# Eight-wide attentions of a twelve-layer decoder: half of the first pair's keys and queries laid by DMA instead of by products, and the rows rearranged for it

## What is computed

```python
q = (queries @ Wq + bq).reshape(b, s, 16, 8)
k = (context @ Wk + bk).reshape(b, p, 16, 8)
v = (context @ Wv + bv).reshape(b, p, 16, 8)
scores = einsum('bqhd,bkhd->bhqk', q, k) / sqrt(8)     # + mask in L0_attn and L1_xattn
out = einsum('bhqk,bkhd->bqhd', softmax(scores), v).reshape(b, s, 128) @ Wo + bo
```

## Time and profile before

| | |
|---|---|
| median of 3 runs | 1826.79 us (1822.91 to 1831.64) |
| the profiled execution, its own time | 1836.73 us |
| its span | 1834.7 us |
| busy PE / DVE / ACT / POOL | 76% / 67% / 50% / 18% of the span |
| granted TensorE clock, mean | 0.878 |

### The profile page before, as it was taken

How to read it: one execution, slowest core, us unless ns; L and a number is a source line. 1 busy time by engine, 2 the same in 40 slices (tenths; PEclk the granted TensorE clock), 3 DMA queues, 4 the chain that set the end, 5 groups by cost and what they waited for, 6 DMA issues and landing times. The chain is left out here.

```text
span 1834.7 us, 31839 instructions
## 1 busy us (share of the span) xinstructions
PE 1388.5 (76%) x10614; PEld 859.6 (47%) x10630; DVE 1235.9 (67%) x4823; ACT 920.4 (50%) x2002; POOL 337.9 (18%) x360
## 2 busy tenths in 40 slices
PE   5897978872874768895455799999983995777874
PEld 2454434441763543442234456666653883443442
DVE  7888368865336768887666677677764224657887
ACT  4654357641322336655622577777751442136666
POOL 3320022112524124400021000000002333303100
PEclk9999999985996879997567799999995997679997
DMA  3230014211561012310010000000003672003300
GB/s 126 55 53 2 0 22 54 36 35 48 164 125 40 12 52 49 51 25 20 1 59 1 12 7 7 12 7 7 1 2 110 186 203 59 23 18 49 55 4 24
DMA packets 59362, 83.42 MB, mean 45 GB/s; under 512 B 8065, under 2 KB 46209, under 8 KB 58689
## 3 DMA queue, kind: packets, MB, share of 16 engines
q1 hardware_dynamic: 54208, 71.15, 15.7%
q0 software_dynamic: 4992, 10.23, 3.0%
HBM read 51.18 MB, written 9.18 MB: 33 GB/s over the span
## 5 line engine op out<-in xcount | busy, mean ns | idle before, releaser
L873 ACT ACTIVATE L_xattn_probs<-ps 128x1024 f32<-128x1024 f32 x192 | 196.5, 1024 | 73.7 <-PE ps L1066 68.9
L714 DVE TENSOR_REDUCE maxs<-ps 128x4 f32<-128x1024 f32 x128 | 156.5, 1222 | 29.7 <-PE ps L1042 29.6
L3467 ACT ACTIVATE wide_pr<-wide_sc,wide_nm 128x256 f32<-128x256 f32 x256 | 127.0, 497 | 13.3 <-DVE wide_nm L3395 12.7
L1543 POOL DMA_INDIRECT moe_xs<-normed,moe_table x92 | 87.1, 947 | 156.7 <-PE ps L1573 73.9
L1042 PE MATMUL ps<-keys,L_xattn_qs 64*128 64x256 bf16 x768 | 75.3, 274 | 53.5 <-DVE maxs L714 33.3
L1082 PE MATMUL ps<-L_xattn_probs,values 128*32 128x256 f32 x1536 | 102.8, 385 | 0.0
L708 DVE CUSTOM_DVE_ANT_0 L_xattn_masked_scores<-ps,L_xattn_maskQ 128x256 bf16<-128x256 f32 x256 | 93.1, 420 | 14.1 <-PE ps L1042 14.1
L3390 DVE COPY wide_prT<-ps 128x512 f32<-128x512 f32 x64 | 44.3, 692 | 84.5 <-PE ps L3508 84.4
L3365 DVE CUSTOM_DVE_ANT_0 wide_sc<-ps,wide_mask 128x256 f32<-128x256 f32 x256 | 93.2, 419 | 3.3 <-PE ps L3493 2.2
L1972 DVE SCALAR_TENSOR_TENSOR moe_z_sb<-ps,moe_wt,moe_a_sb 128x256 f32<-128x256 f32 x46 | 22.3, 484 | 93.4 <-ACT moe_a_sb L2003 78.5
L708 DVE CUSTOM_DVE_ANT_0 L_attn_masked_scores<-ps,L_attn_maskQ 128x128 bf16<-128x128 f32 (+1 forms) x256 | 76.0, 353 | 7.6 <-PE ps L1042 7.2
(11 more groups left out here) (625 smaller groups left out, 3604.9 us busy)
## 6 DMA issues: line engine op xcount, KB each, us to landing
moe_wt<-in_packed_experts SPq DMA_DIRECT2D x23, 707.0 KB
moe_wt<-in_packed_experts SPq DMA_DIRECT2D x23, 384.0 KB
keys<-L_xattn_k_parts SPq DMA_DIRECT2D x108, 64.0 KB
L_xattn_qs<-L_xattn_q_parts SPq DMA_DIRECT2D x108, 64.0 KB
expert_out<-moe_y SPq DMA_DIRECT2D x46, 128.0 KB
weights<-in_packed_L_xattn SPq DMA_DIRECT2D x2, 1316.0 KB, 7.2
keys<-L_attn_k_parts SPq DMA_DIRECT2D x36, 64.0 KB
L_attn_qs<-L_attn_q_parts SPq DMA_DIRECT2D x36, 64.0 KB
```

What stands on the lines that cost most here:

```text
L714: v.tensor_reduce(nm, ps[:, BANK_M:BANK_M + 2, :].rearrange("p j (t n) -> p j t n", t=2), AX.X, ALU.max, negate=True).then_inc(S("m_used"), 1)
L873: a.activation(probs[:, s % RING, :, :, :].rearrange("p j t n -> p j (t n)"), ps[:, BANK_P:BANK_P + 2, :], ACT.Exp, scale=HD ** -0.5)\
L1543: g.indirect_dma_start(self.xs[:, j % BUFS, h * P:(h + 1) * P], None, C.normed, bass.IndirectOffsetOnAxis(self.table[:, n:n + 1], 0))\
L3467: ins = a.activation(pr[:, s % 3, j, qt, :], sc[:, s % 2, j, qt, :], ACT.Exp, bias=nm[:, s % 2, n:n + 1], accum_out=sums[:, s % 2, n:n + 1])
```

## The change

For pair 0, only groups 0 to 3 are placed by products (`PLACED` = 4); groups 4 to 7 of keys and queries are laid by transfers, `lay_keys(sp, 0)` and `lay_queries(sp, 0)`, 12 DMAs each. So that the rows of groups 4 to 7 are contiguous in a part, the column order becomes (head of the group, half of the groups, element, group in its half). A transfer can now cover only 32 contiguous rows for 4 groups; pairs 1 to 3 need both halves, so their layings are 24 DMAs of 32 KB each instead of 12 of 64 KB. Slots 4 to 7 wait for `k_laid` and `q_laid` of 192, and slot 16 m for 192 + 384 m. DVE's copies of keys 4 to 7 and ACT's of queries 4 to 7 go. The spare rows of pair 0's groups 4 to 7 are cleared by two more DMAs in each attention, and set once by two more memsets; the selection matrices are made by 12 copies of half the size instead of 6 on each of DVE and ACT.

```diff
+    PLACED = GP // 2
-    KEY_BANKS = (BANK_P, BANK_P + 1, BANK_T, BANK_V, BANK_P, BANK_P + 1, BANK_P, BANK_P + 1)
-    KEYS_AT = (-2, -2, -1, -1)
+    KEY_BANKS = (BANK_P, BANK_P + 1, BANK_T, BANK_V)
@@ parts_free
-                eng.wait_ge(S(("queries_placed", "keys_placed")[n]), GP)
-            elif m > 2:
-                eng.wait_ge(S(("q_laid", "k_laid")[n]), 192 * (m - 2))
+                eng.wait_ge(S(("queries_placed", "keys_placed")[n]), PLACED)
+            if m >= 2:
+                eng.wait_ge(S(("q_laid", "k_laid")[n]), laid(m - 2))
@@
+        def unplaced(m):
+
+            return range(2) if m else (1,)
+
+        def laid(m):
+
+            return 192 + 384 * m
@@ lay_keys (lay_queries likewise)
-                    eng.dma_start(kk[r0:r0 + HD, m % 2, :, :], parts(m, 1, part)[half[j]]).then_inc(S("k_laid"), 16)
+                    for h in unplaced(m):
+                        rows = slice(64 * j + 32 * h, 64 * j + 32 * h + 32)
+                        eng.dma_start(kk[r0:r0 + HD, m % 2, PLACED * h:PLACED * (h + 1), :], parts(m, 1, part)[rows])\
+                           .then_inc(S("k_laid"), 16)
@@ lay_queries
-            if m == 1:
-                eng.wait_ge(S("rows_cleared"), 32)
+            if m < 2:
+                eng.wait_ge(S("rows_cleared"), 64)
@@ SP queue
                 for m in range(PAIRS):
-                    if m:
-                        lay_keys(sp, m)
+                    lay_keys(sp, m)
                     if boundary is not None:
                         turn_masks(sp, m)
-                    if m:
-                        lay_queries(sp, m)
+                    lay_queries(sp, m)
@@ DVE: copy_key and its two calls are removed
@@ ACT
-                for gp in range(GP // 2):
+                for gp in range(PLACED):
...
-                    if 0 <= s - QUERIES_AT - 1 < GP:
+                    if 0 <= s - QUERIES_AT - 1 < PLACED:
@@ PE, max_scores
                     if s < GP:
-                        pe.wait_ge(S("q_ready"), gp + 1)
+                        query_copied(pe, gp)
                         key_copied(pe, gp)
...
-                            pe.wait_ge(S("k_laid"), 192 * m)
-                            pe.wait_ge(S("q_laid"), 192 * m)
+                            pe.wait_ge(S("k_laid"), laid(m))
+                            pe.wait_ge(S("q_laid"), laid(m))
@@ PE, places
-                    if 0 <= s - QUERIES_AT < GP:
+                    if 0 <= s - QUERIES_AT < PLACED:
                         place_query(s - QUERIES_AT)
-                    for n, t in enumerate(KEYS_AT):
-                        if s == t:
-                            place_key(GP // 2 + n)
@@ decoder
+                L(g.memset(C.keys[96:128, 0, HEADS // 4:, :], 1.0))
...
+                L.tick(v.memset(C.keys[32:64, 0, HEADS // 4:, :], 1.0))
...
-                for slot in range(len(K_PARTS)):
-                    dst, one = lay_rows(1, slot)
+                for slot, h in product(range(len(K_PARTS)), range(2)):
+                    dst, one = lay_rows(1, slot, h)
                     L.tick(v.tensor_copy(dst, one))
@@ by_rows
-    return np.ascontiguousarray(wt.reshape(wt.shape[0], HEADS // 2, 2, HD).transpose(0, 2, 3, 1)).reshape(wt.shape)
+    return np.ascontiguousarray(wt.reshape(wt.shape[0], 2, HEADS // 4, 2, HD).transpose(0, 3, 1, 4, 2)).reshape(wt.shape)
```

More of the change, by code:

```diff
@@ L8 @@
 import itertools
+from itertools import product
 from contextlib import ExitStack, contextmanager
@@ L432, in parts_free, with query_copied @@
             if m == 2:
-                eng.wait_ge(S(("queries_placed", "keys_placed")[n]), GP)
-            elif m > 2:
-                eng.wait_ge(S(("q_laid", "k_laid")[n]), 192 * (m - 2))
+                eng.wait_ge(S(("queries_placed", "keys_placed")[n]), PLACED)
+            if m >= 2:
+                eng.wait_ge(S(("q_laid", "k_laid")[n]), laid(m - 2))
         def key_copied(eng, gp):
-            eng.wait_ge(S("later_keys" if gp >= GP // 2 else "early_keys"), gp % (GP // 2) + 1)
+            if gp < PLACED:
+                eng.wait_ge(S("early_keys"), gp + 1)
+            else:
+                eng.wait_ge(S("k_laid"), laid(0))
+        def query_copied(eng, gp):
+            if gp < PLACED:
+                eng.wait_ge(S("q_ready"), gp + 1)
+            else:
+                eng.wait_ge(S("q_laid"), laid(0))
+        def unplaced(m):
+            return range(2) if m else (1,)
+        def laid(m):
+            return 192 + 384 * m
         places = [Place(tau, WINDOW, PAIRS) for tau in range(-WINDOW, SLOTS + 13)]
@@ L483, in lay_queries @@
                     r0 = 64 * j + HD * part_slot
-                    eng.dma_start(qs[r0:r0 + HD, m % 2, :, :], parts(m, 0, part)[half[j]]).then_inc(S("q_laid"), 16)
+                    for h in unplaced(m):
+                        rows = slice(64 * j + 32 * h, 64 * j + 32 * h + 32)
+                        eng.dma_start(qs[r0:r0 + HD, m % 2, PLACED * h:PLACED * (h + 1), :], parts(m, 0, part)[rows])\
+                           .then_inc(S("q_laid"), 16)
         with C.turn() as block:
@@ L496, in _ @@
                     load_weights(C, sp, ks[at + 1], packed)
[L497 to L500, removed]
+                for m in range(2):
+                    for j in range(2):
+                        r, g0 = slice(64 * j + AUG, 64 * j + 64), PLACED * unplaced(m)[0]
+                        sp.dma_start(qs[r, m, g0:GP, :], bcast(C.c("zeros").bitcast(BF16)[r], 1,
+                                                               [64 - AUG, GP - g0, PAIR]))\
+                          .then_inc(S("rows_cleared"), 16)
                 if boundary is not None:
@@ L1249, in _ @@
                     if 0 <= s - 1 < SLOTS:
-                        if s == 1:
-                            key_copied(pe, GP - 1)
                         prob_scores(s - 1)
-                    if 0 <= s - QUERIES_AT < GP:
+                    if 0 <= s - QUERIES_AT < PLACED:
                         place_query(s - QUERIES_AT)
-                    for n, t in enumerate(KEYS_AT):
-                        if s == t:
-                            place_key(GP // 2 + n)
                     for _ in side:
@@ L3597, in decoder, with lay_rows @@
         C.normed, C.expert_out = normed, expert_out
-        def lay_rows(n, slot):
+        def lay_rows(n, slot, h):
             part = (Q_PARTS, K_PARTS)[n][slot]
-            dst = C.lay[:, n, part, :, :].rearrange("p g (j r) -> p g j r", r=64)
-            return (dst[:, :, :, HD * slot:HD * (slot + 1)],
-                    C.ident.rearrange("p (j d g) -> p g j d", j=2, d=HD))
+            g0 = h * HEADS // 4
+            dst = C.lay[:, n, part, g0:g0 + HEADS // 4, :].rearrange("p g (j r) -> p g j r", r=64)
+            one = C.ident.rearrange("p (j h n) -> p j h n", j=2, h=2)[:, :, h, :]
+            return dst[:, :, :, HD * slot:HD * (slot + 1)], one.rearrange("p j (d g) -> p g j d", d=HD)
         with C.turn() as block:
@@ L3642, in _ @@
                 a.wait_ge(C.sem("lay_cleared"), 2)
-                for slot in range(len(Q_PARTS)):
-                    dst, one = lay_rows(0, slot)
+                for slot, h in product(range(len(Q_PARTS)), range(2)):
+                    dst, one = lay_rows(0, slot, h)
                     L.tick(a.activation(dst, one, ACT.Copy))
```

21 lines of the change are left out of this document (4 added, 17 removed).

## The result

The changed kernel takes **1947.12 us** (median of four runs, 1944.98 to 1949.39), the kernel before beside it 1827.03 (1822.91 to 1831.64): ratio **1.067**, interval 1.0652 to 1.0688. The direction was right; the size was not: 1918 was forecast, with a range up to 1945.

A forecast was written before the change was run, and what follows sets the result against it. It took the PE and its partner engines as pacing each attention, any hold-up of `max_scores` paid in full; 47.0 + 31.4 + 1.2 + 12 = 91.6 us on the 1826.8 median gave 1918 us, range 1893 to 1935, whole range 1868 to 1945.

The forecast's parts named there:

- what one costs is bounded: A 32 KB laying issue on the SP queue: at most 0.68 us, at least 0.39; 0.68 taken.
- pair 1's key parts later: Slot 4's wait in pair 0 delays pair 1's key parts 2.2 us in L0_attn and L0_xattn, 0 in the others.
- slot 16(m-1) to the next layings: Pairs 2 and 3: keys start 7.0 us after the slot in L0_attn, 2.4 and 2.5 in L0_xattn; 34.4 us follow.
- clock, by itself: Half-rate PE clock after twelve stands over 4 us: 1 us each, +12 in all; bounds 0 and 35.
- the 78.4 booked for the pairs: Later slots from the SP queue's 48 issues: +47.0 us in pair 1, +31.4 in pairs 2 and 3.
- The line on L1_xattn: Pairs 2 and 3 of L1_xattn: the new 39.0 us against today's 38.9 between starting slots, so no cost.
- 6.2 us of PE time: Removed placing products, four keys and four queries per attention: 6.2 us, most before or among the first slots, on the path.
- I cost them at nothing of their own: Removed copies, DVE 4 and ACT 4 per attention: no gain of their own, covered by the products of the same places.
- rival 1: Transfers, not issues, pace the SP queue: slot 16 keeps its place, each attention gains 4.5 us; 1810 us, chance 0.06.
- 2 (a cheaper half): A half-size issue on the SP queue is somewhat cheaper, say 0.55 us: 1853 us, chance 0.10.
- 3 (only pair 1 costs): Waits of pairs 2 and 3 hide, only pair 1's 47.0 us and small terms count: 1883 us, chance 0.09.
- 4 (the clock in full): Each of twelve stands costs 2.9 us of clock instead of 1, +23: 1941 us, chance 0.15.

The follow-up runs named there:

- The two experiments with one part each: Kernel before with only pairs 1 to 3 in half-size pieces: 1939.07 us; changed kernel with pairs 1 to 3 back in 12 pieces of 64 KB: 1836.37 us.
- the fillers: Changed kernel with filler products of constants on the PE ahead of the waits at slots 4, 16, 32 and 48: 1942.45 us, ratio 1.0637.
- the shapes: Changed kernel with pairs 1 to 3 in 64 KB pieces again, but layings of L0_xattn and L3_xattn cut into several shapes: 1975.85 us, run once.
- the second queue: Changed kernel with half of the query layings issued from POOL's queue, same 32 KB transfers: 1855.27 us, ratio 1.0132.

## Why the prediction was wrong in size and right in kind

**What held.** One mechanism, in its places: slots 4, 16, 32 and 48; 12 and 24 issues; landing 1.65 us behind the last issue (1.7 taken); preparation +1.6, by the first placed key of L0_attn (28.80 before, 30.36 after; 1.2 taken); slot 4 of L0_xattn 3.6 us later relative to slot 0 (3.0 taken). The two experiments with one part each put 111.5 us on pairs 1 to 3 and 8.8 on pair 0.

**The step that failed** is "what one costs is bounded: above by today's 0.68 us ... I take 0.68". A transfer of half the rows is not at most as dear as a whole one. Line 493 of the changed kernel, durations of single issues in ns, against 599/613/1228 in the earlier trace rows:
```profile
L493 SPq DMA_DIRECT2D keys<-L_xattn_k_parts x252: 657/672/1287, 289.6 to 1839.5; - x126
```
With the gap between two, that is 17.09 / 24 = 0.712 us each, and with the longer ones among them 48 issues took 34.8 us in the mean of the twelve pairs (0.725 each), where I had 32.7. That is 2.1 x 12 = **25 us**, the largest of the terms missed, and it came in full, since the queue sets all twelve slots. The upper bound was read off the wrong shape: "only layings copy within SBUF" was a reason for 0.68 as the value, and none for 0.68 as the end.

**The smaller terms**, booked and measured:

| term | booked | measured |
|---|---|---|
| pair 1's key parts later (sum of four) | 4.4 | 10.8 |
| slot 16(m-1) to the next layings (sum of eight) | 30.6 | 37.8 |
| L1_xattn, pair 3: interval today | 39 (not read) | 37.0 |
| after slot 48 (sum of four) | 0 | 5.2 |
| clock, by itself | 12 | inside the rows above, about 5 by the fillers |

The excesses are 6.4, 7.2, 2.0 and 5.2. With the 25 of the issues and the 78.4 booked for the pairs they make some 124 us, and the attentions grew by 123.4. The 12 us for the clock stood for part of the same: booked and then found under other names. That the miss was only 29 us is in part luck: without these 12 the forecast would have been 1906, and the miss 41. The line on L1_xattn ("nothing") failed twice: 39.0 against 38.9 was no margin once an issue cost more, and slot 48 was not read at all; its pairs 2 and 3 cost 3.5 + 5.2 us.

**A step that cost nothing here but was false**: "6.2 us of PE time, most of it before or among the first slots and on the path there". With the waits gone as well the whole removal yields 3 us for each attention. "I cost them at nothing of their own", of DVE's copies, is in doubt with it: in the first slots DVE was the busier engine (10.18 of 10.40 us). I had read the PE's rows there and not DVE's. So even with the data for free the idea could give 0.65%, and no version tried here that computes all heads beats the kernel before.

**A premise that fitted only the new size**: that slot 16 of L0_xattn waited for issues in the kernel before. It came 5.6 us after the last issue and waited for the data, as rival 1 had noted; the 1.7 us from issue to landing hold for the 32 KB pieces (1.65 measured), so the sum did not suffer.

**The rivals.** 1 (transfers pace the queue) fell for the halved pieces, with the shapes and with the second queue; it describes the kernel before. 2 (a cheaper half) fell: the half is dearer. 3 (only pair 1 costs) fell: the stretches from slot 16 to 48 grew by 58.6 us together, those from slot 0 to 16 by 59.6. 4 (the clock in full) gave the number nearest to the result, 1941, but not the reason: fillers that restore the clock take back 5 us and not 23.

What stays open: why 32 or 16 source rows cost more to issue than 64. No run here separates the number of source rows from the number of groups that one transfer writes in each partition.

## What to carry to other kernels

Count the issues that one queue must make between the time at which data is ready and the time at which it is needed, and multiply by the issue time of that very shape; halving the pieces of a transfer that a queue already makes just in time doubles the time of its issues, and the bytes in each play no part in that. Look as well at whether the data keeps up with the issues: here it did at 32 KB a piece and not at 64. When an edit to one case (pair 0) changes a layout that all cases share, price the others first: here they were 93% of the loss. A second queue cures an issue-bound stretch only if its engine has time to spare and can start early enough, and a queue on POOL has a price at the next barrier.

## What the runs showed of the hardware

- Issue time of SBUF-to-SBUF transfers on the SP queue: 613 ns for 64 rows at 64, 32 and 16 KB; 662 to 672 ns for 32 and for 16 rows. About 40 ns lie between two.
- The same 32-row transfer issued elsewhere: 544 ns on POOL, 707 ns (681 to 774) on ACT in the cross-attentions, where the engine's own work stands meanwhile.
- Each transfer issued from POOL made its DRAIN ahead of the next barrier 82 to 84 ns longer: 6.92 us for 84, 3.50 for 42, 3.00 for 36 at the end of L0_attn.
- The data of 32 KB pieces was used 1.65 to 1.67 us after the last issue ended, in three kernels. With 64 KB pieces it was 5.6 us, and 74 GB/s still moved after the last issue.
- In L0_xattn a granted clock of 0.89 instead of 0.98 cost about 1 us of 163, net of what the fillers held up.
